# Local attention on one NeuronCore: the value copy moves to VectorE, a query rotation moves within VectorE's slot, a query projection moves within TensorE's slot

## What is computed

```python
def _layer(x, wqkv, qs, ksc, wo, lg, lb, w1, b1, w2, b2):
    h = shift_token(x)
    q, k, v = jnp.split(h @ wqkv, 3, axis=-1)
    q, k, v = (to_heads(q), to_heads(k), to_heads(v))      # 8 heads of 64
    q = l2norm(q) * qs
    k = l2norm(k) * ksc
    q, k = rotary_xpos(q, k)
    o = local_attention(q, k, v)    # windows of 64, each sees itself and the one before
    x = x + o.transpose(0, 2, 1, 3).reshape(b, n, INNER) @ wo
    h = layernorm(shift_token(x)) * lg + lb
    a, g = jnp.split(h @ w1 + b1, 2, axis=-1)
    return x + (a * gelu(g)) @ w2 + b2
```

## Time and profile before

| what | value |
|---|---|
| runs | 1383.84, 1385.69 and 1386.09 us, median 1385.69 us |
| the profiled execution | 1383.86 us, of which the span is 1382.0 us |
| busy over the span | PE 86%, DVE 68%, ACT 65%, POOL 42% |
| slots 0 to 11 of layer 0 | 990.45 to 1097.30 us, 106.85 us |
| slots 0 to 11 of layer 1 | 1195.42 to 1302.26 us, 106.84 us |
| length of one such slot | 8.91 us |

### The profile page before, as it was taken

The page is one execution under the profiler, slowest core; times in us unless marked ns, Lnnn a source line. Parts: engine busy times, 40 slices in busy tenths (PEclk is TensorE's granted clock), DMA queues, the critical chain, the costliest instruction groups (busy, mean ns, idle before and its releaser), DMA issues.

```text
span 1382.0 us, 28209 instructions
## 1 busy us (share of the span) xinstructions
PE 1194.7 (86%) x10484; PEld 703.7 (51%) x10484; DVE 936.2 (68%) x2300; ACT 895.3 (65%) x2352; POOL 575.8 (42%) x554
## 2 busy tenths in 40 slices
PE   8777048758999999999979899998799978899978
PEld 5333048743555555555524466664466643466643
DVE  3454842247989889889863799997666744666733
ACT  4664001116777777777757888886698962689961
POOL 1022035525444444444230122222888820888820
PEclk8997558879999999999999999999999999999998
DMA  9002105531000000000020000000111100011100
GB/s 335 3 0 61 55 18 187 165 89 50 1 1 1 1 1 1 1 1 2 1 107 0 1 2 2 2 2 20 29 29 29 29 15 0 22 29 23 29 14 30
DMA packets 25797, 48.03 MB, mean 35 GB/s; under 512 B 4883, under 2 KB 16667, under 8 KB 25022
## 3 DMA queue, kind: packets, MB, share of 16 engines
q1 hardware_dynamic: 23614, 44.49, 10.1%
q0 software_dynamic: 2048, 1.74, 0.5%
HBM read 33.17 MB, written 6.55 MB: 29 GB/s over the span
## 4 chain that ended last, share of the span: by engine, by line
PE 68%; ACT 13%; DVE 9%; issue 5%; another core or an unknown queue 2%; POOL 2%; DMA 1%; SPq 0%; ACTq 0%; DVEq 0%; POOLq 0%
ACT win_soft_local L1582 7%; PE bank L1115 6%; PE bank L1128 5%; PE pair L1084 4%; PE bank L1548 4%; PE bank L1536 4%; PE bank L1102 3%; PE bank L2341 3%; PE pair L1102 3%; PE bank L1562 3%; PE bank L1570 3%; PE pair L1087 2%; PE pair L1805 2%; ACT win_sq_local L2129 2%; PE bank L2041 2%
## 5 line engine op out<-in xcount | busy, mean ns | idle before, releaser
L1370 POOL TENSOR_TENSOR rope_part<-rope_part,rope_tab 128x512 f32<-128x512 f32 x64 | 81.5, 1274 | 189.2 <-DVE rope_part L1276 189.1
L2269 POOL TENSOR_TENSOR win_part<-win_part,scaled_tab 128x512 f32<-128x512 f32 x64 | 91.9, 1436 | 63.6 <-DVE win_part L2206 63.4
L1203 ACT ACTIVATE soft<-bank,neg_max 128x512 f32<-128x512 f32 (+2 forms) x192 | 100.3, 535 | 27.5 <-DVE neg_max L1284 27.3
L1582 ACT ACTIVATE win_soft_local<-bank,win_neg_max_local,rq 128x128 f32<-128x128 f32 x256 | 114.1, 475 | 0.1
L1621 POOL TENSOR_TENSOR win_soft_alibi<-win_soft_alibi,win_inv_alibi 128x384 f32<-128x384 f32 x64 | 51.7, 826 | 147.9 <-DVE win_inv_alibi L1605 147.8
L1220 ACT ACTIVATE softT<-bank 128x512 f32<-128x512 f32 x160 | 92.5, 599 | 29.5 <-PE bank L1115 29.4
L1284 DVE CUSTOM_DVE_ANT_0 bank<-bank,att_mask 128x512 f32<-128x512 f32 (+2 forms) x192 | 92.3, 523 | 6.9 <-PE bank L1102 6.9
L1102 PE MATMUL bank<-k_rope,q_rope 64*128 64x512 f32 (+3 forms) x384 | 95.3, 473 | 1.6 <-POOL k_rope L1375 1.6
L1115 PE MATMUL bank<-ident,soft 128*128 128x128 f32 x640 | 89.4, 278 | 0.6 <-ACT softT L1220 0.5
L1314 DVE TENSOR_SCALAR soft<-soft,exp_inv 128x128 f32<-128x128 f32 (+2 forms) x160 | 87.4, 594 | 1.1
L1115 PEld LDWEIGHTS bank<-ident,soft 128*128 128x128 f32 x640 | 70.6, 140 | 32.6 <-issue 17.7
(11 more groups left out here) (404 smaller groups left out, 3351.7 us busy)
## 6 DMA issues: line engine op xcount, KB each, us to landing
moe_w<-in_moe_w SPq DMA_DIRECT2D x8, 960.0 KB
y_tok<-in_moe_w SPq DMA_DIRECT2D x8, 960.0 KB
v_even<-v_odd SPq DMA_DIRECT2D x32, 128.0 KB, 2.2
v_even<-v_odd SPq DMA_DIRECT2D x32, 96.0 KB, 2.2
y_dram<-zeros SPq DMA_DIRECT2D x8, 256.0 KB
htok_dram<-htok SPq DMA_DIRECT2D x2, 1024.0 KB
y_tok<-y_dram SPq DMA_DIRECT2D x8, 256.0 KB, 4.8
att_w<-in_att_w SPq DMA_DIRECT2D x1, 1536.0 KB, 8.1
```

What stands on the lines that cost most here:

```text
L1203: nc.scalar.activation(soft[par][:, hd, TILE_AT[t]:TILE_AT[t] + keys(t)], score_bank(u, s, hd)[:, at:at + keys(t)], ACT.Exp, scale=-1.0, b ...
L1370: nc.gpsimd.tensor_tensor(rope_part[2 * piece + 1][:, :], rope_part[2 * piece + 1][:, :], rope_tab[:, 2 * piece + 1, :], ALU.mult).then_in ...
L1582: nc.scalar.activation(a["soft"][u % 2][:, j, :], tile, ACT.Exp, bias=low, scale=rq[:, u % 2, j:j + 1], accum_out=a["sum"][:, u % 2, j:j + ...
L2269: nc.gpsimd.tensor_tensor(swapped, swapped, scaled_tab[:, 2 * j + 1, :], ALU.mult) \
```

## The change

On ACT `take_values(s + 2)` is gone; DVE does it as a `tensor_copy` with the same waits and the same semaphore, between its two `inverse` steps. DVE's `rotate` of a query, formerly `rotate(s + 3, 0)` as the first step of a slot, is now `rotate(s + 4, 0)` between the two `inverse` steps of the slot before. On PE `project(s + 4, 0)`, which stood behind `transpose(s, 1)`, now stands ahead of it. SP's DMAs, POOL's list and all sizes are the same.

```diff
@@ local_pe
                 on(W, transpose, s, 0)
                 on(W, project, s + 3, 1)
+                on(W, project, s + 4, 0)
                 on(W, transpose, s, 1)
-                on(W, project, s + 4, 0)
                 on(W, key_sums, s + 3)
@@ local_act
-            def take_values(u):
-                act.wait_ge(sem("win_v_raw"), W.at("win_v_raw", u, 1))
-                if u >= 3:
-                    act.wait_ge(sem("pv_raw"), W.at("pv_raw", u, -2))
-                tiles = bank[5][:, :].rearrange("p (i c) -> p i c", i=TB)
-                nc.scalar.activation(v_odd[u % 3][:, :, :], tiles, ACT.Copy).then_inc(sem("win_v_read"), 1)
                 on(W, key_root, s + 3)
-                on(W, take_values, s + 2)
                 on(W, query_root, s + 3)
@@ local_dve
+            def take_values(u):
+                dve.wait_ge(sem("win_v_raw"), W.at("win_v_raw", u, 1))
+                if u >= 3:
+                    dve.wait_ge(sem("pv_raw"), W.at("pv_raw", u, -2))
+                tiles = bank[5][:, :].rearrange("p (i c) -> p i c", i=TB)
+                nc.vector.tensor_copy(v_odd[u % 3][:, :, :], tiles).then_inc(sem("win_v_read"), 1)
@@ local_dve, the loop
-                on(W, rotate, s + 3, 0)
                 on(W, maxes, s + 1, 0)
@@
                 on(W, inverse, s + 1, 0)
+                on(W, rotate, s + 4, 0)
+                on(W, take_values, s + 2)
                 on(W, inverse, s + 1, 1)
```

## The result

The changed kernel takes 1393.94 us (median of 5 runs, 1389.62 to 1398.88) against 1385.69 us (5 runs) for the kernel before. The ratio is 1.0063 with a 95% interval of 1.0036 to 1.0089: slower by 5 to 12 us. The direction was forecast, the size was not: +17.1 us and no less than 1396 were expected, and about +8.7 came. In the runs further down a few executions lay 2% or more above the rest of their kernel; they are in the medians given here and not in the ratios.

A forecast was written before the change was run, and what follows sets the result against it. The prediction took the latency of one PE-then-ACT loop as the bound, not any engine's work. It summed +20.2 and -3.1 to +17.1 us, giving 1402.0 us, range 1396 to 1409.5.

The forecast's parts named there:

- The bound: Slots 0 to 11: the latency of one loop of waits through PE (some 3.5 us) and ACT (5.3 us) sets the slot.
- The swap: PE, slots 0 to 11: query projection ahead of second transposes delays the second evacuation 0.84 us; 24 x 0.84 = +20.2 us.
- Rival 2: Slots: the two effects nearly cancel, putting the projection ahead costing under 0.25 us a slot; 1383 to 1388 us; chance 0.05.
- The rotation: DVE's query rotation one step earlier removes 0.12 us of issue before PE's query sums, slots 0 to 12: -3.1 us.
- The value copy: Moved from ACT to DVE between the inverses: worth 0, with 1 us of slack or more on DVE.
- Fill and tail: Slots -4 to -1 and 12 to 15: taken as 0, with 0.6 us either way for each layer.
- Rival 3, the clock: TensorE's clock falls in the longer slots, 1.7 us lost each; about 1412 us, or 1443 if in every slot; chance 0.05.
- The sum: Whole kernel: 20.2 - 3.1 = +17.1 us, giving 1402.0 us.

The follow-up runs named there:

- the last experiment: Whole change, plus the query sums waiting again for the scores ahead of them on TensorE, against the kernel before: 1410.02 against 1385.08 us, ratio 1.0168.

## Why the prediction was right and wrong

**The bound: right.** The loop of the earlier trace rows is what sets the slot. Removing 0.48 us of ScalarE's work changed nothing (8.91 us with the value copy alone), and moving one copy in ScalarE's order took the whole cost of the swap away (8.45 us with the swap, 8.44 without).

**The swap: right mechanism, term too large.** 24 x 0.84 = +20.2 was forecast, 24 x 0.69 = +16.6 measured, twice (8.91 to 9.60, and 8.56 to 9.25). The step that failed is the sentence that the key projection covers the wait for bank 7 to the end. I had taken the records' ends: the projection's modelled end, 1242.42 + 1.02, meets the transposes' start at 1243.42. But products that follow a projection with nothing to wait for start 0.86 us after its start, not 1.02; so the query projection would have started at 1243.28 and not, as I wrote, at about 1243.46. From 1243.28 to 1243.42 the transposes were waiting for ScalarE's copy, whose 0.60 us end at 1243.28 and whose semaphore TensorE acted on 0.14 later. The query projection filled that hole. Rival 2 had named just this, that the emptying is what the second transposes really wait for, and I turned it down by the same recorded end; the wait is there, but it is too short to cancel the two effects.

**The rotation: the term that was mis-sized most.** -3.1 us was forecast, with 0.12 us a slot and 0.19 as the bound. Measured is 8.91 - 8.56 = 0.35, in slots 0 to 11 and 0.34 in slot 12: -9.1 us (6 to 12) by the ratio of the run with it alone. The failing step is that I priced the wait by the gap of 0.12 us that the chain shows ahead of the sums. That gap is counted from the scores' recorded end, and it is again the recorded end that misled: with the wait met early the sums start 0.20 us ahead of that end. They had been held for 0.32 us (1.22 against 0.90 after the scores' start), and the group itself took 0.03 more. The bound of 0.19 came from the earlier trace rows, where the transposes behind the scores start 1.03 us after the scores' start; I took the same for the sums, which can start after 0.90. The prediction cited the Trainium skill, "TensorE: Matmul & The Clock Gate", section "Step-by-step: what each phase is for", for the order of the matmuls, and drew nothing from what it names beside it, that weight loads may be pulled ahead of running matmuls. The weight loads of the run with the rotation alone agree with it (first load at 1206.88, scores until 1207.19), and the idle of 0.39 us in the last experiment shows that a wait not yet met stops it. The statement ahead of the prediction that each engine executes its list in order is too strong for these weight loads.

**The value copy: right.** 0 was forecast and 8.91 us measured. That VectorE would have 1 us of slack or more held too: its second inverse came at 1221.23, and its maxima then waited for the scores.

**Fill and tail: right within their bound for the whole change** (slot -1 within 0.03 us, slot 12 -0.34 each by the rotation). The copy without the rotation costs 0.9 us a layer, more than the 0.6 that I allowed.

**Rival 3, the clock: half right.** In the profile of the changed kernel the clock is 1.00 in all 24 slots. It did fall in slots of 9.60 and 9.66 us. Of slots 2 to 11 of both layers, none was longer than its kernel's usual length in the nine profiles with slots of 8.44 to 9.25 us, and 2, 1 and 3 slots were in the three profiles with 9.60 and 9.66. Had the slot been as long as I forecast, the forecast would have lacked this term: these falls took 1.7 to 5.1 us in the three profiles. The price of 1.7 us each was right (11.29 against 9.60, 11.35 against 9.66). The 1.73 us that I set against 0.86 was a recorded length set against a distance of starts; the recorded length at full clock is 1.02. What in those slots the clock answered to is open: TensorE's idle ahead of the mask products is 1.09 to 1.10 us at 9.25 and at 9.60 alike, and the longer slots have the late query sums besides. The granted clock also was low (0.69 to 0.85) in slot 0 or 1 of a layer in seven of the twelve profiles, with and without the swap, so that a single profile's total differs by 1.5 to 5 us in the kernels with slots up to 9.25 us, and by up to 7.6 in the swap alone, for a reason that these runs do not tell.

**The sum.** By the measured terms: 24 x 0.69 - 26 x 0.35 = 16.6 - 9.1 = +7.5 us, against 17.1 forecast and +8.7 (5 to 12) measured. The two terms missed by 3.6 and 6.0 us, both the same way and both because a wait was measured from a recorded end. The range missed because its lower end held the first term at 0.84 us and allowed the second no more than 0.19; either term as measured would have brought 1393.94 into it. The direction came out right because the swap is the larger term in either sum.

## What to carry to other kernels

On TensorE a semaphore that is met "just in time", at the recorded end of the group before, is late: the query sums could start 0.20 us ahead of that end. Where a group of short matmuls follows a wait, let the wait be met while the group before still runs, and price a late one from the start of the group before to the start of the waiting one. Ask of each step on an in-order engine who needs it next; here a copy that its reader needed only some 2 us later stood ahead of the exponentials on which the loop turned, and putting it behind the first four was worth 0.80 us a slot in the changed kernel, and 0.12 us without the swap, where its input came early. And read the throughput of matmuls from start to start: their recorded ends hid a wait of 0.14 us and most of one of 0.32 here.

## What the runs showed of the hardware

- Two 512 column products follow each other at 0.43 us, but each record is 0.59 us and a pair of them 1.02; a group that starts 1.00 us after the pair's start has waited 0.14 us although its record starts where the pair's ends.
- A wait met at the end of the group before costs the query sums 0.35 to 0.41 us (8.56 against 8.91, 9.25 against 9.66 us), of which only 0.12 to 0.18 shows as a gap ahead of them. While the wait is not met, their weight loads do not start either (0.34 to 0.39 us of idle).
- TensorE starts the waiting transposes 0.14 us after the recorded end of ScalarE's emptying, with or without other products between (slots 0, 5 and 14 of layer 1).
- TensorE's clock fell to its lower level within 6 of the 60 slots 2 to 11 of the three profiles with slots of 9.60 and 9.66 us, at 1.69 us of lost time each, and in none of the 180 of the nine profiles with 8.44 to 9.25 us. Why is open.
